# Wide attention scores that accumulate onto those of two key tiles before, and maxima from bf16 copies of keys and queries

## The reference, cut to what matters

```
def _L1_xattn_ref(query, context, w_q, w_kv, w_out, b_out):   # 1024 x 128 and 6404 x 96
    q = query @ w_q                                            # 1024 x (16 heads of 64)
    k, v = jnp.split(context @ w_kv, 2, axis=-1)               # 6404 x (16 heads of 64), each
    ...
    scores = jnp.einsum('bhqd,bhkd->bhqk', q, k) * 64 ** -0.5
    attn = jax.nn.softmax(scores, axis=-1)
    out = jnp.einsum('bhqk,bhkd->bhqd', attn, v)
    ...
    return out @ w_out + b_out
```

## Time and profile before

| | |
|---|---|
| median of three runs | 3855.21 us |
| span of the profiled execution (the only time that it has) | 3852.1 us |
| TensorE matmul busy | 3585.8 us, 93% |
| VectorE busy | 2721.2 us, 71% |
| GpSimd busy | 2367.2 us, 61% |
| ScalarE busy | 2164.0 us, 56% |
| mean granted TensorE clock | 0.977 |

### The profile page before, as it was taken

The page is one execution under the profiler, slowest core; times in us unless marked ns, Lnnn a source line. Parts: engine busy times, 40 slices in busy tenths (PEclk is TensorE's granted clock), DMA queues, the critical chain, the costliest instruction groups (busy, mean ns, idle before and its releaser), DMA issues.

```text
span 3852.1 us, 61024 instructions
## 1 busy us (share of the span) xinstructions
PE 3585.8 (93%) x23264; PEld 1471.9 (38%) x23264; DVE 2721.2 (71%) x4447; ACT 2164.0 (56%) x2535; POOL 2367.2 (61%) x1280
## 2 busy tenths in 40 slices
PE   6868999999999999889999999999999999999999
PEld 2332222222222244334444444444444444444444
DVE  5758888888888547776766666667666676666742
ACT  4667888888888744644444444444444444444422
POOL 3115656566565303047888888888788888889810
PEclk7969999999999999999999999999999999999999
DMA  4220001010001002500111000101010010012100
GB/s 132 52 44 8 1 10 27 1 26 11 1 1 43 10 5 87 204 14 25 29 29 29 27 28 27 30 25 32 26 29 27 28 29 28 25 55 71 30 0 6
DMA packets 74058, 126.73 MB, mean 33 GB/s; under 512 B 9875, under 2 KB 26341, under 8 KB 73093
## 3 DMA queue, kind: packets, MB, share of 16 engines
q1 hardware_dynamic: 73772, 122.82, 11.2%
HBM read 88.15 MB, written 34.64 MB: 32 GB/s over the span
## 4 chain that ended last, share of the span: by engine, by line
PE 51%; DVE 4%; ACT 2%; issue 1%; DVEq 0%; ACTq 0%
PE PS L2371 20%; PE PS L2345 12%; PE PS L2300 6%; PE PS L2358 5%; PE PS L2318 3%; DVE att_top_piece L2555 2%; DVE att_k_lo L2569 2%; PE PS L340 1%; PE PS L348 1%; PE PS L341 1%; ACT att_k_hi L2463 1%; PE PS L2311 0%; PE PS L2329 0%; PE PS L2323 0%; DVE att_prob L2535 0%
## 5 line engine op out<-in xcount | busy, mean ns | idle before, releaser
L2220 POOL TENSOR_TENSOR att_total<-att_total,att_prob 128x1024 f32<-128x1024 f32 x597 | 1543.7, 2586 | 352.4 <-ACT att_prob L2484 304.5
L2484 ACT ACTIVATE att_prob<-PS 128x1024 f32<-128x1024 f32 x816 | 790.9, 1021 | 1005.1 <-PE PS L2358 1005.1
L2555 DVE TENSOR_REDUCE att_top_piece<-PS 128x1 f32<-128x512 f32 (+1 forms) x1560 | 971.8, 664 | 349.6 <-PE PS L2300 339.8
L1878 DVE TENSOR_REDUCE att_top_piece<-PS 128x1 f32<-128x512 f32 (+1 forms) x1459 | 904.9, 664 | 132.4 <-PE PS L1591 127.0
L1781 ACT ACTIVATE att_prob<-PS 128x1024 f32<-128x1024 f32 (+2 forms) x912 | 892.0, 1004 | 173.5 <-PE PS L1623 170.6
L2371 PE MATMUL PS<-att_prob,att_vals 128*64 128x512 f32 x3264 | 792.0, 605 | 3.7 <-issue 2.9
L1646 PE MATMUL PS<-att_prob,cross_Vst 128*32 128x256 f32 (+1 forms) x5544 | 506.5, 431 | 2.7 <-issue 0.8
L1493 POOL TENSOR_TENSOR att_stage<-att_stage,att_run 128x512 f32<-128x512 f32 x150 | 191.4, 1276 | 401.9 <-ACT att_stage L1760 401.6
L2300 PE MATMUL PS<-att_k_hi,att_q_hi 64*128 64x512 f32 (+1 forms) x1664 | 376.3, 449 | 60.3 <-DVE att_top_piece L2555 47.0
L1591 PE MATMUL PS<-cross_Kstack,cross_Qmax 49*128 49x512 bf16 (+1 forms) x1664 | 323.5, 386 | 95.1 <-DVE att_top_piece L1878 33.4
L2345 PE MATMUL PS<-att_q_hi,att_k_hi 64*128 64x512 f32 x1632 | 329.1, 396 | 0.0
(11 more groups left out here) (316 smaller groups left out, 3394.6 us busy)
## 6 DMA issues: line engine op xcount, KB each, us to landing
att_vals<-values SPq DMA_DIRECT2D x192, 256.0 KB, 2.6
values<-att_prob SPq DMA_DIRECT2D x14, 1024.0 KB, 4.1
values<-cross_Vall SPq DMA_DIRECT2D x10, 1024.0 KB, 4.2
cross_Kstack<-kparts SPq DMA_DIRECT2D x36, 204.0 KB
f_w<-in_f_w SPq DMA_DIRECT2D x24, 256.0 KB, 3.7
kparts<-cross_Vst SPq DMA_DIRECT2D x24, 128.0 KB, 1.8
att_vals<-values SPq DMA_DIRECT2D x16, 192.0 KB, 2.3
k_ctxT<-in_ctxT SPq DMA_DIRECT2D x1, 2448.0 KB
```

Source lines behind the costliest of these rows:

```text
L1878: dve.tensor_reduce(top_piece[:, n % 2, s * QT + qt, c:c + 1], PS[:, banks[item][s], 0:w], AX, ALU.max).then_inc(dve_freed, 1)
L2220: pool.tensor_tensor(so_far, so_far, prob[0:rows, j % RING, :, :], ALU.add).then_inc(summed, 1)
L2484: act.activation(prob[:, j % RING, :, :].rearrange("p a b -> p (a b)"), PSf[:, b:b + 2 * HALF], ACT.Exp, scale=scale).then_inc(exped, 1)
L2555: dve.tensor_reduce(top_piece[:, n % 2, s * QT + qt, c:c + 1], PS[:, bank_of(item, s), 0:w], AX, ALU.max).then_inc(dve_freed, 1)
```

## The change

1. Keys and maxima's inputs. ScalarE writes a chunk k twice from PSUM: as it is, 256 columns later, into `k_raw`, and as bf16 into `k_top`. VectorE then takes `k_step` = key minus the key 256 columns (two tiles) before. A round later ScalarE rounds `k_step` to `k_hi` (`round_hi`), and a further round later VectorE leaves `k_lo` = `k_step` - `k_hi` (`leave_lo`). The first 256 columns are the keys themselves. `k_raw` and `k_step` lie in the memory of `k_hi` and `k_lo`. An item q gets a bf16 copy as well (`q_top`).
2. Scores. From the third key tile of a unit on, the products with `k_hi` and `k_lo` are added to what the bank holds, which are the scores of tile t-2, maxima already taken off. So the maxima's products are left for tiles 0 and 1 of each unit, and a step tells ScalarE by its last product.
3. An m item multiplies `q_top` with `k_top` (bf16). Where its two banks lie side by side, one reduction of 128 x 1024 serves both heads and frees both banks at its end.
4. VectorE takes every third step's sum from 7 on in place of every fourth, in all units but the last.
5. Chunks stop at column 6404, and GpSimd clears the columns after it once, at the start. The program's DMA scratch size is set to 1024.

```diff
-                pe.wait_ge(dve_freed, dve_count[("k", p, kt // 4)])
+                pe.wait_ge(lo_left, lo_number[("k", p, kt // 4)])
...
-                for k, q, start in ((k_hi, q_hi, True), (k_hi, q_lo, False), (k_lo, q_hi, False)):
+                for k, q, last in ((k_hi, q_hi, False), (k_hi, q_lo, False), (k_lo, q_hi, kt >= 2)):
                     for s in range(2):
-                        pe.matmul(PS[:, b + s, :], k[p % 2][strip(s), keys], q[n % QBUFS][strip(s), :],
-                                  start=start, stop=False, tile_position=(s * DH2, 0))
+                        i = pe.matmul(PS[:, b + s, :], k[p % 2][strip(s), keys], q[n % QBUFS][strip(s), :],
+                                      start=kt < 2 and k is k_hi and q is q_hi, stop=last,
+                                      tile_position=(s * DH2, 0), skip_group_check=kt >= 2)
+                if kt >= 2:
+                    i.then_inc(scored, 1)
...
                 score(j)
+                if j % KT == 1:
+                    subtract_maxima(j)
                 score(j + 1)
+                if j % KT == 0:
+                    subtract_maxima(j)
+                if (j + 1) % KT < 2:
+                    subtract_maxima(j + 1)
                 for item in early[j // 2]:
                     side(item)
-                subtract_maxima(j)
...
-                        ins = pe.matmul(PS[:, bank_of(item, s), 0:w], q_hi[n % QBUFS][strip(s), qt * P:(qt + 1) * P],
-                                        k_hi[p % 2][strip(s), c * HALF:c * HALF + w], start=True, stop=True,
+                        ins = pe.matmul(PS[:, bank_of(item, s), 0:w], q_top[strip(s), n % 2, qt * P:(qt + 1) * P],
+                                        k_top[strip(s), c * HALF:c * HALF + w], start=True, stop=True,
...
                 if kind == "q":
-                    act.activation(q_hi[n % QBUFS][:, :], PS[:, bank_of(item), :], ACT.Copy).then_inc(hi_copied, 1)
+                    act.activation(q_hi[n % QBUFS][:, :], PS[:, bank_of(item), :], ACT.Copy)
+                    act.activation(q_top[:, n % 2, :], PS[:, bank_of(item), :], ACT.Copy).then_inc(kept, 1)
                 elif kind == "k":
-                    c = chunk(item[2])
-                    act.activation(k_hi[n % 2][:, c], PS[:, bank_of(item), 0:c.stop - c.start], ACT.Copy
-                                   ).then_inc(hi_copied, 1)
+                    c, to = chunk(item[2]), later_columns(item[2])
+                    act.activation(k_raw[n % 2][:, to], PS[:, bank_of(item), 0:to.stop - to.start], ACT.Copy)
+                    act.activation(k_top[:, c], PS[:, bank_of(item), 0:c.stop - c.start], ACT.Copy).then_inc(kept, 1)
...
+            def round_hi(item):
+                c = chunk(item[2])
+                act.wait_ge(dve_freed, dve_count[item])
+                act.activation(k_hi[item[1] % 2][:, c], k_step[item[1] % 2][:, c], ACT.Copy
+                               ).then_inc(hi_rounded, 1)
...
+                    pieces = top_piece[:, n % 2, :, :].rearrange("p (s t) c -> p s t c", s=2)
+                    if adjacent(item):
+                        b = bank_of(item)
+                        dve.tensor_reduce(pieces[:, :, qt, c], PS[:, b:b + 2, 0:w], AX, ALU.max).then_inc(dve_freed, 2)
+                    for s in range(0 if adjacent(item) else 2):
+                        dve.tensor_reduce(pieces[:, s, qt, c:c + 1], PS[:, bank_of(item, s), 0:w], AX,
                                           ALU.max).then_inc(dve_freed, 1)
...
-                    dve.wait_ge(hi_copied, hi_count[item])
-                    dve.tensor_tensor(k_lo[n % 2][:, c], PS[:, bank_of(item), 0:c.stop - c.start],
-                                      k_hi[n % 2][:, c].bitcast(F32), ALU.subtract).then_inc(dve_freed, 1)
+                    lead = PAIR if item[2] == 0 else 0
+                    dve.wait_ge(kept, hi_count[item])
+                    if lead:
+                        dve.tensor_copy(k_step[n % 2][:, 0:lead], PS[:, bank_of(item), 0:lead])
+                    rest = slice(c.start + lead, c.stop)
+                    dve.tensor_tensor(k_step[n % 2][:, rest], PS[:, bank_of(item), lead:c.stop - c.start],
+                                      k_raw[n % 2][:, rest], ALU.subtract).then_inc(dve_freed, 1)
...
+            def leave_lo(item):
+                c, p = chunk(item[2]), item[1]
+                dve.wait_ge(hi_rounded, hi_number[item])
+                dve.tensor_tensor(k_lo[p % 2][:, c], k_step[p % 2][:, c], k_hi[p % 2][:, c].bitcast(F32),
+                                  ALU.subtract).then_inc(lo_left, 1)
...
-                for item in whole[j // 2] + late[j // 2]:
+                for item in whole[j // 2]:
+                    side(item)
+                for item in lo_of[j // 2]:
+                    leave_lo(item)
+                for item in late[j // 2]:
                     side(item)
...
     def dve_adds(j):
-        return j % KT % (2 if j // KT == LAST else 4) == (1 if j // KT == LAST else 3) and 7 <= j % KT
+        if j // KT == LAST:
+            return j % KT % 2 == 1 and 7 <= j % KT
+        return j % KT % 3 == 1 and 7 <= j % KT
```

92 lines of the change are left out of this document (61 added, 31 removed).

## The result

The changed kernel takes **4047.18 us** (median of four runs, 4045.45 to 4058.11) against 3856.24 for the kernel before on the same chip: ratio 1.0502, 95% interval 1.0479 to 1.0525. It is 5% slower. Forecast were 3843 us and a range of 3778 to 3905, with faster as the likeliest outcome (0.41); time, range and direction are wrong. The profiled execution has a span of 4045.6 us and a mean granted clock of 0.955 (before 0.977).

A forecast was written before the change was run, and what follows sets the result against it. TensorE was taken to bound the kernel almost everywhere, with VectorE following closely. Unit savings of -41.5 us plus 29 us of extra costs gave -12.5, a span of 3839.6 and a forecast of 3843 us, range 3778 to 3905.

The forecast's parts named there:

- the meeting is mostly avoided: Wide attention: VectorE's and GpSimd's sums seldom meet since GpSimd waits for the same exponentials; VectorE's sum priced at 1.21 us.
- paired reductions: Maxima reductions: one instruction of 1.22 us, first bank back after 1.27 us instead of 0.83, two of three items paired.
- second copy in the key chain: Rounds with keys or queries: VectorE waits for two ScalarE copies of 0.60 us instead of one; such rounds +0.36 us.
- `leave_lo` at 0.61 us: VectorE's low part of keys: +0.27 us in even units' rounds with a sum, hidden in odd units.
- first score later: Start of wide attention: second copies 13 x 0.6, two for q, about 2 us for rounding and `lo`: +11 us.
- rival B: VectorE's sums slowed by meeting GpSimd's, each +0.85 us: 3962 us, or 3903 if half meet; chance 0.20.
- rival C: Granted clock falls as TensorE waits more; 1% lost in the steps is 20 us: 3863 us; chance 0.05.
- The subtraction: TensorE's subtraction of maxima: 1632 matmuls become 64, a slot worth 0.44 us a round, against a 0.32 us shape change.
- Maxima in bf16: TensorE's maxima products: weight load 93 ns against 185, taking 0.09 us off from late to next early maxima item.
- Rival A: VectorE follows TensorE better, paired banks and key chain costing nothing extra: 3723 us, 3761 with second copy paid; chance 0.22.
- Unit 14: Wide attention's unit without keys: two reciprocal rounds, 13 with a sum, 10.5 plain ones, together -8 us.
- The last unit: Wide attention's final unit, which has no maxima items: 25 x -0.44 us, so -11 us.

## Why the prediction was wrong, and where it was right

The steps, as the prediction put them. The amounts are differences of medians and overlap where two causes share a round.

| step of the prediction | priced | measured |
|---|---|---|
| sums, "each 1.21 us where it runs undisturbed"; "the meeting is mostly avoided" | 0 | 2149 ns a sum; ordering alone is worth 113 us in the change and 73 with single reductions, taking out nearly all the work too 127 |
| paired reductions, mean of 3.81 and 3.89 in plain rounds, of 3.81 and 4.16 with a sum, of 6.02 and 6.46 with keys | about 60 us of cost within the prices | 142 us in the change, 101 with GpSimd ordered, 109 in the kernel before |
| second copy in the key chain, 0.60 of it | at most 0.60 x 105 = 63 us | 38 us |
| `leave_lo` at 0.61 us, +0.27 where it meets a sum | some 25 us | 1133 ns; 49 us by its place |
| first score later | +11 | +16.4 |
| unit 0 | +4 | +26 (171.4 us against 145.3; 151 with single reductions and shortened sums) |
| granted clock in the steps 1.00 | 0 | 0.97, and 0.96 from 2050 to 2550 us; 0.99 and 1.00 once the pairing is undone |

The rounds themselves, E to E, say where it was lost. Medians in us of the rounds between 1852 and 3400 us of each trace (in the change 60, 47, 30, 30 and 49 rounds), by what VectorE does in them:

| VectorE, beside the reductions | priced | change | single reductions | and GpSimd behind the sums | and `leave_lo` behind them |
|---|---|---|---|---|---|
| nothing | 3.86 | 4.06 | 3.81 | 3.81 | 3.81 |
| a sum | 4.04 | 5.04 | 4.48 | 4.21 | 3.82 |
| `leave_lo` | 3.86 ("hidden") | 5.41 | 4.67 | 4.68 | 4.67 |
| a sum and `leave_lo` | 4.62 | 5.75 | 5.41 | 4.20 | 4.20 |
| a difference of keys, with or without a sum | 6.31 | 6.4 | 5.9 | 5.9 | 5.9 |

The prices of rounds with keys and of plain ones were near; those of the rounds with a sum or with `leave_lo` were 1.0 to 1.6 us too low.

**The step that failed first** is one sentence under rival B: "Now the meeting is mostly avoided: GpSimd waits for the same exponentials." It set the price of a meeting at nothing, for sums and, as "hidden", for `leave_lo`. For the kernel before it was nearly true (30 of 171 sums start inside one of GpSimd's), but it was carried over to the changed one, where 189 of 231 do. The removed subtraction is also what held the exponentials back behind E. Without it they come 1.64 us earlier against E (from +0.88 to -0.76), and GpSimd, which waits for nothing else, comes forward with them, while VectorE still does E's reductions first. B had the right mechanism and near enough the right size (0.85 us a sum priced, 2149 - 1210 = 939 ns measured), but was given 0.20 and set apart from the forecast. It should have been the forecast, though its 3962 us are 85 too low as well, since pairing came on top. Both signs that the prediction named for B and C are there, sums over 1.5 us and a clock below 1.00. The meeting could be read from the trace of before: GpSimd's sum is 3.14 us long where VectorE was in first and 2.36 where not. And a timeline of the round, redrawn without the 0.44 us of subtraction, puts GpSimd first.

**The second** is the price of pairing. The mechanism was right (the first bank comes back at the end of both), and so was the place. The sizes were not: 1.87 us from L to E where 0.43 + 1.27 = 1.70 had been priced. The 0.43 was read from the earlier trace rows, where a reduction takes one bank; one that takes two starts when both strips' products are there, after 0.50. The 1.27 came from the earlier trace rows; in the steps it is 1.37. That is 0.17 us in two of three plain rounds, and where VectorE comes late, the whole difference of 0.54 us (1.37 - 0.83) falls on TensorE. With a sum or `leave_lo` in the round it often was late. So the two costs feed each other: pairing costs 142 us with the collision and 101 with most of it gone.

**What the two leave.** The forecast for the span was 3839.6, measured are 4045.6: 206 us too little. By stretch of the trace, without overlap, the change is over the kernel before by 16 us at the first score, 26 in unit 0, 154 in units 1 to 13 and -2 in the last two, with -1 behind them. By cause, undoing the pairing and putting GpSimd behind both the sums and `leave_lo` takes 264 us off (4047.18 to 3783.42), in steps of 142, 73 and 49. About 60 of them, the pairing, had been priced, so some 204 are what the forecast lacked, which is all of the miss (4047 - 3843). That it comes out so closely is luck, since some collisions are left in that kernel and start and unit 0 were off by themselves.

**The clock** (rival C) fell as it had been described, with TensorE waiting more, and rose to 1.00 in the middle when the reductions were single again (TensorE busy 433 of 500 us there in place of 417). What it costs in the steps was not isolated, but it is bounded: from 1680 to 3840 us the mean grant is 0.97 (before 1.00), and if the grant is either full or half, as the shorter and longer rows of one shape suggest, 110 to 150 of these 2160 us are at half (an estimate), which costs 75 us at most and less where TensorE waits anyway. The 109 us of pairing in the kernel before and most of the 73 of the ordering come at a grant of 0.99 or 1.00 in the steps, so the clock is not their cause; of the 142 us it may hold a part. At the start it does show. The product of a chunk of keys, before (first row) and in the change, where the grant is 0.50 from 1640 to 1664 us:

```profile
1627.42 1.13 PE L2318 MATMUL PS<-k_ctxT,k_wk 96*128 96x512 f32 x2
```
```profile
1629.20 2.07 PE L2357 MATMUL PS<-k_ctxT,k_wk 96*128 96x512 f32 x2
```

A chunk then takes 4.71 us (1629.20 to 1633.91) in place of 3.53, where 0.60 more had been priced; that is enough for the 5 us over the price there.

**What held.** The subtraction: 64 matmuls left, and E to L of 2.19 us. Maxima in bf16: L to E of 1.62 us, 0.8% by itself in the kernel before (3827.11). The plain round of 3.81 us, 2.19 + 1.62, is the median one once the reductions are single. Rival A's "VectorE follows" was out of reach with the order as it was. Unit 14, priced at 8 us less than the 114.1 of before, took 116.8 in the change, 115.5 with single reductions and 108.3 with GpSimd behind the sums, which is the price within 2 us: the loss there is nearly all collision. The last unit came down 4.4 us (101.5 to 97.1) where 11 were priced; with shortened sums it takes 91.1, so what is missing lies in VectorE's sums of every second step. Waiting or work was not told apart there: with GpSimd behind them it still takes 97.5. Third-step sums cost nothing in the kernel before, as reasoned.

**What stays open.** Why fourth-step sums are slower than third-step ones in the change (4172.95 against 4047.18) was not settled: more of them meet a sum of GpSimd (159 of 171 sums, 73 of 104 `leave_lo`, against 189 of 231 and 38 of 104), and the granted clock from 2050 to 2550 us is 0.93 in place of 0.96. Why the phase falls so was not found, nor the share of the clock. Open is also the round with `leave_lo` alone, which stays at 4.67 us in the last column above: GpSimd is still in the middle of a sum in some of them (`leave_lo` of 2.46 us at 2118.34).

The removed subtraction, the accumulating scores and the bf16 maxima stand. With single reductions, GpSimd behind VectorE, `leave_lo` behind the sums and one copy in the chain this is the best version found, 3743.51 us, and 84 us under the best one tried that keeps the subtraction (3827.11).

## What to carry to other kernels

When work is taken off the engine that bounds a kernel, redraw one round and ask of every pair of engines that get in each other's way who now comes first: here VectorE's sums, its copies from SBUF and `leave_lo`, with all their inputs in SBUF, stand behind GpSimd's running sum. Make the engine with room to spare wait for the other, with one semaphore. One instruction for two banks saves an issue but gives both banks back at its end; use it only where nobody waits for the first bank. And where a mean duration is made of long and short ones (GpSimd's 2592 ns here, of 2.36 and 3.14 us), look at both before taking a price from it.

## What the runs showed of the hardware that was not expected

- A VectorE add with both inputs in SBUF that starts inside a GpSimd sum of 2.36 us ends at a fixed time after it: 1.08 us for 128 x 1024, 0.02 us for 128 x 2 (medians). The profile counts the wait as the instruction's own duration and names no releaser. The small one lasts 994 ns on average in one order and 201 ns in the other; the full one up to 3.41 us, in a round with keys of the change:

```profile
2615.61 3.41 DVE L2676 TENSOR_TENSOR k_xn<-k_xn,att_prob 128x1024 f32<-128x1024 f32 x1
2618.94 0.68 DVE L2627 TENSOR_TENSOR att_k_step<-PS,att_k_raw 128x512 f32<-128x512 f32 x1
```

- The difference with one input in PSUM takes 0.62 to 0.70 us in every order tried (128 x 512, 88 in each trace), while `leave_lo`, of the same size with both in SBUF, goes from 0.68 to means of 1.0 to 1.9 us. The Trainium skill (SBUF — State Buffer, "Who interferes with whom") makes the same distinction: a VectorE instruction with at most one SBUF input, outside certain modes, does not contend with GpSimd, one with two does.
- A reduction over two banks gives TensorE the first of them 1.37 us after its start, two reductions of one bank each after 0.83 us.
